# Attention stage: weights in 32 pieces shared with POOL, a new order in the turns, and no filler products

## The reference, cut to what matters

```python
t = jnp.einsum('bshd,hde->bshe', xh, Wqk)                 # 16 heads of 16, Wqk = tril @ tril.T
scores = jnp.einsum('bshe,bthe->bhst', t, xh) / jnp.sqrt(d)
attn = jax.nn.softmax(scores, axis=-1)
Vh = (x @ Wv.T + bv).reshape(bs, seq_len, H, d)
out = jnp.einsum('bhst,bthd->bshd', attn, Vh).reshape(bs, seq_len, emb_dim)
return out @ Wo.T + bo
# later, for each of 8 experts e, with w1[e] 256 x 1024 and w2[e] 1024 x 256:
h = jax.nn.relu(xt @ w1[e] + b1[e]); y = h @ w2[e] + b2[e]
```

## Time and profile before

| | |
|---|---|
| three runs | 1568.89, 1578.52, 1579.11 us; median 1578.52 |
| the profiled execution: its own time | 1564.47 us |
| its span | 1562.7 us |
| mean granted clock of PE in it | 0.823 of full speed |
| PE, DVE, ACT, POOL busy | 1102.0, 1083.2, 680.0, 455.6 us (71%, 69%, 44%, 29%) |
| attention stage | about 1124 to 1330 us of the span |
| longest DMA queue | q1: 67.97 MB, 13.9% of 16 engines |

### The profile page before, as it was taken

The page is one execution under the profiler, slowest core; times in us unless marked ns, Lnnn a source line. Parts: engine busy times, 40 slices in busy tenths (PEclk is TensorE's granted clock), DMA queues, the critical chain, the costliest instruction groups (busy, mean ns, idle before and its releaser), DMA issues. The chain is left out here.

```text
span 1562.7 us, 31816 instructions
## 1 busy us (share of the span) xinstructions
PE 1102.0 (71%) x9968; PEld 766.5 (49%) x9968; DVE 1083.2 (69%) x2356; ACT 680.0 (44%) x1360; POOL 455.6 (29%) x607
## 2 busy tenths in 40 slices
PE   4515877774299997776667868266489887469991
PEld 2212222224188884554445745144456665458881
DVE  3867999997555555657967754888667777745553
ACT  4515555553265553214426622244256665244440
POOL 0051777772154544710001100000033333222203
PEclk9557999995599998887977977688588888579996
DMA  6500000001344554302000000000012322112213
GB/s 209 199 4 11 0 1 0 1 1 48 95 123 135 162 130 146 93 19 81 1 0 1 1 1 0 0 1 0 29 56 83 110 83 82 48 45 63 63 53 118
DMA packets 45461, 89.68 MB, mean 57 GB/s; under 512 B 8096, under 2 KB 34373, under 8 KB 42437
## 3 DMA queue, kind: packets, MB, share of 16 engines
q1 hardware_dynamic: 38274, 67.97, 13.9%
q0 software_dynamic: 6912, 18.88, 4.2%
q10 hardware_dynamic: 144, 1.05, 0.2%
HBM read 71.84 MB, written 16.04 MB: 56 GB/s over the span
## 5 line engine op out<-in xcount | busy, mean ns | idle before, releaser
L909 POOL TENSOR_TENSOR scan_ch<-scan_hs,scan_ct 128x452 f32<-128x452 f32 x128 | 143.5, 1142 | 82.0 <-DVE scan_hs L1019 53.4
L932 PE MATMUL scan_py<-scan_ch,ident 128*128 128x452 f32 x256 | 131.2, 602 | 41.0 <-POOL scan_ch L909 31.3
L1019 DVE TENSOR_TENSOR_SCAN scan_hs<-scan_abar,scan_bx 128x452 f32<-128x452 f32 x128 | 132.8, 1077 | 0.8 <-ACT scan_abar L981 0.4
L2620 POOL TENSOR_TENSOR mha_prob_lo<-mha_prob,mha_prob_hi 113x452 f16<-113x452 f32 x64 | 65.5, 1046 | 129.8 <-ACT mha_prob_hi L2788 129.8
L458 PE MATMUL m0x_ph<-m0x_xb,m_w_hi 128*128 128x128 f16 x456 | 99.3, 219 | 0.5 <-ACT m0x_xb L1625 0.4
L459 PE MATMUL m0x_ph<-m0x_xb,m_w_hi 128*128 128x128 f16 x456 | 99.2, 219 | 0.0
L460 PE MATMUL m0x_ph<-m0x_xb,m_w_lo 128*128 128x128 f16 x456 | 98.8, 218 | 0.0
L1690 DVE TENSOR_SCALAR m3x_a<-m3x_ph,m3x_b 128x128 f32<-128x128 f32 x184 | 49.7, 342 | 68.0 <-ACT m3x_ah L1651 68.0
L932 PEld LDWEIGHTS scan_py<-scan_ch,ident 128*128 128x128 f32 x256 | 40.5, 193 | 112.6 <-POOL scan_ch L909 103.9
L981 ACT ACTIVATE scan_abar<-ssm_dt,ssm_a 128x448 f32<-128x448 f32 x128 | 80.9, 638 | 23.9 <-DVE scan_hs L1019 22.4
L1687 DVE SCALAR_TENSOR_TENSOR m0x_a<-m0x_ph,m0x_b,m0x_gate 128x128 f32<-128x128 f32 x114 | 34.7, 346 | 71.4 <-ACT m0x_gate L1635 67.7
(11 more groups left out here) (677 smaller groups left out, 3825.3 us busy)
## 6 DMA issues: line engine op xcount, KB each, us to landing
mha_wbuf<-m3w SPq DMA_DIRECT2D x16, 1024.0 KB, 4.7
tok_wbuf<-m0w SPq DMA_DIRECT2D x15, 768.0 KB, 4.2
m0x_b<-m0b SPq DMA_DIRECT2D x57, 128.0 KB, 3.5
m_out<-m0x_yo SPq DMA_DIRECT2D x57, 128.0 KB
m3x_b<-m3b SPq DMA_DIRECT2D x23, 128.0 KB, 3.2
m_out<-m3x_yo SPq DMA_DIRECT2D x23, 128.0 KB, 1.7
m_rows<-m0r_parts SPq DMA_DIRECT2D x4, 448.0 KB
m_rows<-m3r_parts SPq DMA_DIRECT2D x4, 448.0 KB
```

The source lines that it names most:

```text
L909: pool.tensor_tensor(ch[r][:], hs[r][:], ct[n % 2][:], ALU.mult).then_inc(weighed, 1)
L932: pe.matmul(py[c][:, 0:GT], core.ident[:], ch[u % R][:], start=n == 0, stop=n == NS - 1).then_inc(summed, 1)
L1019: dve.tensor_tensor_scan(hs[u % R][:], abar[c][:, 0:GT], bx[u % R][:], 0.0, ALU.mult, ALU.add).then_inc(scanned, 1)
L2620: pool.tensor_tensor(prob_lo[g][:], prob[g % 2][:], prob_hi[g][:], ALU.subtract).then_inc(p_low, 1)
```

## The change

The weights of the experts now go in 32 pieces of 512 KB through three buffers (`CutWeights`), two pieces a turn. ACT rounds both at the end of its turn. Of the even piece DVE makes the low half as before, at the start of its next turn. For the odd one ACT also multiplies the buffer in place by the scale (`scale`), and POOL makes the low half as the difference (`low_scaled`), after the four low halves of `prob`. POOL's and SP's loops are written out instead of looped.

The order of PE's, ACT's and DVE's turns changes: DVE takes the maxima of the next batch before anything of this one; PE runs `project_u` and the second call of `first_pass` ahead of `weigh_v`, and `project_out` after `project_v` and `turn_peaks`; ACT takes v before it rounds the probabilities, takes q before the third exponential, and takes the weights last. `project_v` now waits for the addition of one batch earlier, and `take_v` waits for the addition that `project_v` waited for. `keep_warm` is gone, with its 14 products a turn. The core of the diff:

```diff
--- before.py
+++ after.py
@@ -1108,6 +1108,10 @@
         self.small, self.ready = st.sem("small_landed"), st.sem("mult_ready")
         self.w1h, self.w1l, self.w2h, self.w2l = (w[:].rearrange("p e k n -> p e (k n)")
                                                   for w in (m.w1_hi, m.w1_lo, m.w2_hi, m.w2_lo))
+        self.small_tiles(st)
+
+    def small_tiles(self, st):
+        m = self.m
         if m.mult:
             self.gain = st.sb("gain", [128, m.E, m.FH])
         self.router = st.sb("router", [128, KC * m.E])
@@ -1170,6 +1174,58 @@
             ins = dve.scalar_tensor_tensor(dst, src.rearrange("p (a n) -> p a n", a=1),
                                            WS if g is None else g, hi, ALU.mult, ALU.subtract)
         ins.then_inc(self.lo_done[b], 1)
+
+
+class CutWeights(MoeWeights):
+
+
+
+
+
+    CUTS = 2
+
+    def __init__(self, st, m, d, depth):
+        self.m, self.d, self.depth = m, d, depth
+        self.cols = KC * m.NF * 128 // self.CUTS
+        self.buf = [st.sb(f"wbuf{p}", [128, self.cols]) for p in range(depth)]
+        self.landed, self.lo_done = ([st.sem(f"w_{n}{p}") for p in range(depth)] for n in ("landed", "lo"))
+        self.hi_done, self.scaled = st.sem("w_hi"), st.sem("w_scaled")
+        self.small, self.ready = st.sem("small_landed"), st.sem("mult_ready")
+        self.w1h, self.w1l, self.w2h, self.w2l = (w[:].rearrange("p e k n -> p e (k n)")
+                                                  for w in (m.w1_hi, m.w1_lo, m.w2_hi, m.w2_lo))
+        self.small_tiles(st)
+        self.pieces = m.E * 2 * self.CUTS
+
+    def place(self, n, w1, w2):
+        whole, cut = divmod(n, self.CUTS)
+        expert, half = divmod(whole, 2)
+        return (w1, w2)[half][:, expert, cut * self.cols:(cut + 1) * self.cols]
+
+    def load(self, sp, n):
+        whole, cut = divmod(n, self.CUTS)
+        need(sp, self.lo_done[n % self.depth], n // self.depth)
+        sp.dma_start(self.buf[n % self.depth][:], self.d[self.m.name + "w"][:, whole, cut * self.cols:(cut + 1) * self.cols]
+                     ).then_inc(self.landed[n % self.depth], 16)
+
+    def high(self, act, n):
+        act.wait_ge(self.landed[n % self.depth], n // self.depth * 16 + 16)
+        act.activation(self.place(n, self.w1h, self.w2h), self.buf[n % self.depth][:], ACT.Copy,
+                       scale=WS).then_inc(self.hi_done, 1)
+
+    def scale(self, act, n):
+        act.wait_ge(self.hi_done, n + 1)
+        act.activation(self.buf[n % self.depth][:], self.buf[n % self.depth][:], ACT.Copy, scale=WS).then_inc(self.scaled, 1)
+
+    def low(self, dve, n):
+        dve.wait_ge(self.hi_done, n + 1)
+        dve.scalar_tensor_tensor(self.place(n, self.w1l, self.w2l), self.buf[n % self.depth][:], WS,
+                                 self.place(n, self.w1h, self.w2h), ALU.mult,
+                                 ALU.subtract).then_inc(self.lo_done[n % self.depth], 1)
+
+    def low_scaled(self, pool, n, before):
+        pool.wait_ge(self.scaled, before + 1)
+        pool.tensor_tensor(self.place(n, self.w1l, self.w2l), self.buf[n % self.depth][:],
+                           self.place(n, self.w1h, self.w2h), ALU.subtract).then_inc(self.lo_done[n % self.depth], 1)
 
 
 def stage_route(nc, core, m):
@@ -2584,8 +2640,8 @@
         s1, s2 = ([st.ps(f"{n}{r}", [L, 512]) for r in two] for n in ("s1", "s2"))
         pacc, pt = st.ps("pacc", [128, 512]), st.ps("pt", [128, 512])
         v_high, p_high, p_low = st.sem("v_high"), st.sem("p_high"), st.sem("p_low")
-        mw = MoeWeights(st, m, d, 1)
-        assert m.steps == NB
+        mw = CutWeights(st, m, d, 3)
+        assert mw.pieces == 2 * NB
         (ones_set, u_ready, q_ready, ac_ready, v_ready, v_out, s1_ready, maxed, peaks_ready, mt_ready,
          qm_ready, am_ready, s2_ready, exped, pv_done, rec_ready, o_made, oh_ready, ol_ready, out_ready,
          h_added) = (st.sem(n) for n in (
@@ -2605,7 +2661,8 @@
             @block.sync
             def _(sp):
                 mw.load_small(sp)
-                steps(sp, m.steps, lambda at: mw.load(sp, at))
+                for n in range(mw.pieces):
+                    mw.load(sp, n)
 
             @block.gpsimd
             def _(pool):
@@ -2614,11 +2671,12 @@
                 pool.wait_ge(ones_set, 3)
                 pool.memset(unit[:, :, 0:HD], 1.0).then_inc(ones_set, 1)
 
-                with pool.Fori(0, NB) as j:
+                for j in range(NB):
                     for g in range(4):
                         pool.wait_ge(p_high, j * 4 + (g + 1))
                         pool.tensor_tensor(prob_lo[g][:], prob[g % 2][:], prob_hi[g][:],
                                            ALU.subtract).then_inc(p_low, 1)
+                    mw.low_scaled(pool, 2 * j + 1, j)
 
             @block.tensor
             def _(pe):
@@ -2634,7 +2692,7 @@
                 def project_v(j):
 
                     need(pe, v_out, j)
-                    need(pe, h_added, j - 1)
+                    need(pe, h_added, j - 2)
                     cols = bass.ds(j * L, L)
                     for k in range(KC):
                         mm3(pe, pvo[:, 0, :], core.xt_hi[:, k, cols], core.xt_lo[:, k, cols], wv_hi[:, k, :],
@@ -2714,11 +2772,6 @@
                     pe.matmul(pvo[:, 1, :], core.ones16[0:1, 0:L], bo_lo[:], start=False,
                               stop=True).then_inc(out_ready, 1)
 
-                def keep_warm(n):
-
-                    for _ in range(n):
-                        pe.matmul(pt[:, 128:512], core.xt_hi[:, 0, 0:128], core.xt_hi[:, 1, 0:384], start=True, stop=True)
-
                 def prologue():
                     project_u(0)
                     project_v(0)
@@ -2734,22 +2787,19 @@
                     if ahead1:
                         first_pass(j + 1, 1 - p, 0)
                     if now:
-                        keep_warm(5)
                         second_pass(j, p, 2)
-                        keep_warm(9)
+                    if ahead2:
+                        project_u(j + 2)
+                    if ahead1:
+                        first_pass(j + 1, 1 - p, 2)
                     if now:
                         weigh_v(j, p, 0)
                         weigh_v(j, p, 1)
+                    if ahead1:
+                        project_v(j + 1)
+                        turn_peaks(j + 1)
                     if behind:
                         project_out(j - 1)
-                    if ahead1:
-                        first_pass(j + 1, 1 - p, 2)
-                    if ahead2:
-                        project_u(j + 2)
-                    if ahead1:
-                        project_v(j + 1)
-                    if ahead1:
-                        turn_peaks(j + 1)
                     if now:
                         weigh_v(j, p, 2)
                         weigh_v(j, p, 3)
@@ -2766,6 +2816,7 @@
                 def take_v(j):
                     act.wait_ge(v_ready, j + 1)
 
+                    need(act, h_added, j - 1)
                     need(act, pv_done, j * 4)
                     act.activation(v_hi[:, :, 0:HD], pvo[:, 0, :].rearrange("p (h e) -> p h e", e=HD), ACT.Copy,
                                    scale=1.0 / WS).then_inc(v_high, 1)
@@ -2802,25 +2853,29 @@
                     if now:
                         exponential(j, 0)
                         exponential(j, 1)
+                        if j == 0:
+                            act.wait_ge(ones_set, 4)
+                        take_v(j)
                         round_prob(j, 0)
                         round_prob(j, 1)
-                        if isinstance(j, int) and j == 0:
-                            act.wait_ge(ones_set, 4)
-                        take_v(j)
+                    if ahead2:
+                        take_q(j + 2)
+                    if now:
+                        exponential(j, 2)
+                        exponential(j, 3)
                     if behind:
                         take_o(j - 1)
                     if now:
-                        exponential(j, 2)
-                        exponential(j, 3)
                         round_prob(j, 2)
                         round_prob(j, 3)
-                        if isinstance(j, int) and j == 0:
-                            act.wait_ge(mw.ready, 2)
-                        mw.high(act, at)
-                    if ahead2:
-                        take_q(j + 2)
                     if ahead1:
                         take_qm(j + 1)
+                    if now:
+                        if j == 0:
+                            act.wait_ge(mw.ready, 2)
+                        mw.high(act, 2 * j)
+                        mw.high(act, 2 * j + 1)
+                        mw.scale(act, 2 * j + 1)
 
                 turns(act, prologue, turn)
 
@@ -2890,26 +2945,26 @@
                 def turn(at, now, ahead1, ahead2, behind):
                     j, p = at.j, at.c % 2
                     if behind:
-                        normalize(j - 1)
```

(19 more changed lines are left out.)

## The result

The changed kernel takes 1581.95 us (median of 20 runs), the kernel before 1576.76 (median of 20, 1568.89 to 1583.36): a ratio of 1.0045, with a 95% interval of 1.0027 to 1.0062. By the ratio it is 7 us slower (0.0045 x 1577): clearly not faster, and well inside the 1% that was called "same". Its profiled execution has a span of 1579.1 us, against 1562.7; 9.1 of these 16.4 us lie ahead of the first exponential of turn 0 (1146.74 against 1137.63), before the attention stage begins, in stages that are the same in both kernels (its first small DMA starts at 1133.59 against 1124.47).

A forecast was written before the change was run, and what follows sets the result against it. The prediction took a refill loop through one weight buffer as the bound; 15 x (11.80 - 10.4) = 21.0 us plus 1.9 for the tail gave 23 us less, 1578.5 to 1555, range 1536 to 1584.

The forecast's parts named there:

- same: Outcome class of the whole kernel's time, within about 1% (16 us): rival 2 and most of Rival 3, chance 0.25.
- The bound before: Attention turn: a closed refill loop through one weight buffer, 11.12 us, sets the turn; no engine fills it.
- The prices: Weight pieces per turn: DVE 1.21 us, POOL 2.17, ACT 1.06 for each of three instructions.
- The turn of 9.3 us at the full clock: Attention turn: loop from ACT's scaling through POOL's piece and remainders to the next scaling, 9.3 us.
- PE's turn at the half clock: Attention on PE at 1.2 GHz: 11.7 us of work plus about 0.5 of waiting, 12.2 us a turn.
- The clock: PE's clock in the attention loop: share of 0.45 at half, giving a mean turn of 10.4 us.
- rival 2: Attention loop: the clock stays at half, turn 12.2 us, 1583 us, no change; chance 0.18.
- The tail: After the last attention turn: half-size weight pieces shorten ACT's rounding and DVE's low half, 1.9 us less.
- Rival 3: DVE's low half waits for all of POOL's piece: 12 us less gain, 1567 us; chance 0.08.
- Rival 4: PE's waits uncovered at half clock: 14.3 us a turn, +36 us, 1614, at half clock throughout; chance 0.09.

The follow-up runs named there:

- e8: e1 with the transposed maxima (turn_peaks) ahead of project_v on PE; 1541.07 us, ratio 0.978 to the kernel before.
- e1: The changed kernel with the 14 unread products put back, 5 before the second second_pass and 9 before weigh_v; 1555.3 us, ratio 0.986 to the kernel before.
- e5: The changed kernel with 9 unread products a turn, before weigh_v only; ratio 1.005 to the kernel before.
- e10: e1 with its 14 unread products on 128 rows by 32 columns of the array; ratio 0.984 to the kernel before.
- e11: e1 with its 14 unread products on 32 rows by 128 columns of the array; ratio 1.0275 to the kernel before.
- e2: The kernel before with only its 14 unread products a turn taken out; ratio 1.003 to the kernel before.
- e4: e1 with its 14 unread products on 32 x 32 of the array; ratio 1.041 to the kernel before.
- e9: The changed kernel, without filler, with the transposed maxima ahead of project_v on PE; ratio 1.008 to the kernel before.
- e7: e1 with both low halves of the weights on DVE, no scaling on ACT and no piece on POOL; ratio 0.997 to the kernel before.
- e13: The changed kernel without filler, ACT's three weight instructions moved behind the fourth exponential, POOL's piece after its second remainder; ratio 1.037 to the kernel before.

## Why the prediction was wrong, point by point

**The bound before** was read rightly. The refill loop of 11.12 us went when its cause went: no ACT row waits for that DMA now. (The 512 KB loads take 3.8 us to land, inside the bounds of 0 and 4.7, and are covered.)

**The prices** of the weight pieces held: DVE 1.22 us for 1.21, POOL 2.12 for 2.17, ACT 1.06.

**The turn of 9.3 us at the full clock** was the right loop (in e8 it is 9.35, with POOL in it), but it wasn't the turn of this change. With the clock held (e1) the turn is 10.08, as `turn_peaks` stands behind `project_v`, which in turn stands behind the second `weigh_v`; I had put that wait of ACT, 0.68 us, at nothing. With it gone (e8) the turn is 9.35.

**PE's turn at the half clock** was put at 11.7 us of work and 0.5 of waiting. It is 12.20 and 0.39. The factor of 1.75 came from one pass. PE's work at the full clock was 6.8 us, not 6.7 (in e1's steady turn 9.42, of which 2.62 are filler), and over the whole turn the factor is 12.2 / 6.8 = 1.8. That is an error of 0.4 us in a turn all at half; the sign doesn't hang on it, since 12.2 is above the 11.80 of before already.

**The clock** is the step that failed, and with it the sign. I took a share of 0.45 of the loop at half, from the loop of the linear attention, and waits of PE "under 1 us". It was 0.96 (a clock of 0.52), and where the clock is full the wait is 1.57 us (e5). What the runs showed in its place: without its 14 filler products this order stays at 1.2 GHz, and with them it is at 0.95 (e1). The row that I took was of a loop whose products stream into 64 to 128 rows; the scores' products here stream into 32, and for fillers e10 and e11 show that this matters. That it is why the clock stayed low is argued from the fillers, not shown, and e2's 0.65 with the same products says that it isn't the whole reason; this cause stays open. The sentence "PE's work is 72% against 82%" counted time, and by time e4 and e11 would have the highest clock of all. The sum with the measured share, 1 / (0.96/12.2 + 0.04/9.3) = 12.05 us, is nearly that of rival 2: 12.2 us a turn, 4 us slower, 1583 us. Measured are 12.34 and 1582, 7 us slower. Rival 2 had 0.18 of the chance. What spoke for it stood in the prediction ("the products that filled PE's queue while the clock was low are gone"), against it that PE would be almost without a gap; that was true, and no help. That 1582 lies within the stated range is no credit to the forecast: the range took in rival 2, and the forecast itself was 23 us faster.

**The tail** was put 1.9 us shorter. From the first exponential of turn 15 to the end of the stage it went from 15.7 to 14.4 us, 1.3 shorter. The loop's 8.1 and this make +6.7, and the timed ratio +7.1.

**Rival 3**, engines that exclude each other, is real, and was put aside too lightly. Its own meeting, DVE's low half with POOL's piece, doesn't happen in the kernel after (1.22 us, over as POOL's piece starts at 1245.53); there the meeting is another and costs 0.2 us a turn off the path. It does happen in e9 (2.33 us), and others in e7 and e13, where they lengthen the turn. The step that put it aside is a misreading: the earlier trace rows were taken for scans with two SBUF operands, but `scan_abar` is a PSUM tile (line 885 of the kernel before), so each scan reads one tensor from SBUF. Those rows show that such a scan isn't held up; of instructions with two SBUF operands they say nothing.

**Rival 4**, PE's waits uncovered at half clock, was not met: one wait of 0.39 us is left in the turn. Its bound of three quarters of the time at half is also too low: a mean turn of 12.9 out of 14.3 and 9.3 needs 0.8.

## What to carry to other kernels

Work that nobody reads can keep TensorE's clock up, and here it was worth more in the better order: take it out last, and by itself (here it gave 0.4 us a turn in the old order, 1.9 in the new one). When TensorE hardly waits any more in a new order, price the loop at both clocks before anything else, with the time of each piece of its work at each clock, and don't take the clock from a loop whose products have another shape. When you move an instruction on VectorE, look at what GpSimd does at that time: subtractions of two SBUF tensors, and in e7 one instruction with a single one, stood there until GpSimd's was done.

## What the runs showed of the hardware

- Fillers that stream the same 384 columns differ: granted clock 0.95 with 128 rows x 128 columns or 128 x 32, 0.52 with 32 x 128 or 32 x 32. TensorE was busy 93% of the loop in the first two (e1, e10) and all of it in the others (e11, e4). Which property of the instruction does it, beyond rows against columns, stays open: only these four shapes were tried.
- A TensorE that was busy 176 of the 185 us of the loop had a granted clock of 0.52 over it, that is 1.2 GHz in nearly all of it (the kernel after). The same products in the old order, busy 150 of 183 us, had 0.65 (e2).
- The clock fell after waits of TensorE of 1.31 us (the kernel before) and 1.57 us (e5).
- VectorE's subtraction of two SBUF tensors waited out GpSimd's: 2.13 us for 0.39 (e13), 2.33 for 1.22 (e9), 1.24 for 0.40 (e7). So did an instruction with one SBUF tensor, 0.99 for 0.23 (`mha_peaks`, e7). The other way round GpSimd's pair took 2.24 for 2.04. VectorE's scan, with one operand in SBUF and one in PSUM, was not held up by GpSimd's products, 2.09 us for two.
- A swap that helps at one clock (0.9 us a turn, e8) gives nothing at the other (e9).
